# Causal attention scores from two rounded parts and two stacked heads, with the stacks loaded through GpSimd's queue

## What is computed

```python
x = x + attn(layernorm(x))
# in attn, for each of 4 batches and 16 heads
q = (xn @ wq + bq) ; k = (xn @ wk + bk) ; v = (xn @ wv + bv)
scores = einsum('bhqd,bhkd->bhqk', q, k) / sqrt(16)     # 1024 x 1024 a head
attn = softmax(scores + causal_mask)
out = einsum('bhqk,bhkd->bhqd', attn, v) @ wo + bo
```

## Time and profile before

| | us |
|---|---|
| median of 3 runs | 2358.67 (2347.09 to 2362.86) |
| the profiled execution | 2356.39 |
| its span, first to last instruction | 2354.7 |
| prepare | 0 to 195 |
| causal_attention | 195 to 769 |
| one group in its steady part | 32.9 |
| mean granted TensorE clock | 0.952 of 2.4 GHz |

### The profile page before, as it was taken

The page is one execution under the profiler, slowest core; times in us unless marked ns, Lnnn a source line. Parts: engine busy times, 40 slices in busy tenths (PEclk is TensorE's granted clock), DMA queues, the critical chain, the costliest instruction groups (busy, mean ns, idle before and its releaser), DMA issues.

```text
span 2354.7 us, 36114 instructions
## 1 busy us (share of the span) xinstructions
PE 2015.3 (86%) x11968; PEld 1253.7 (53%) x11968; DVE 1448.2 (62%) x3942; ACT 1241.8 (53%) x2980; POOL 798.6 (34%) x663
## 2 busy tenths in 40 slices
PE   5566899999988736989989989989989989989988
PEld 3232233333322525666666666656767667657666
DVE  5467677787774435646646746646745745746744
ACT  1121566666667224745754754753754754754663
POOL 2233221112232335505505505614613613613620
PEclk9796899999999868999999999999999999999999
DMA  5646744554530541000000000011100000000000
GB/s 145 153 132 134 141 98 66 82 82 69 103 109 10 158 138 77 1 28 10 1 23 14 1 23 14 1 66 64 49 19 19 19 19 18 19 4 33 19 1 27
DMA packets 124455, 128.97 MB, mean 55 GB/s; under 512 B 50460, under 2 KB 101232, under 8 KB 123248
## 3 DMA queue, kind: packets, MB, share of 16 engines
q1 hardware_dynamic: 123696, 117.75, 21.6%
q0 software_dynamic: 576, 8.91, 1.0%
HBM read 75.51 MB, written 50.86 MB: 54 GB/s over the span
## 4 chain that ended last, share of the span: by engine, by line
PE 35%; DVE 13%; ACT 8%; issue 6%; POOL 2%; DMA 0%; DVEq 0%; SPq 0%; POOLq 0%; ACTq 0%
DVE rot_s L1862 5%; PE qkv_ps L1372 5%; PE s_ps L1412 4%; PE qkv_ps L1313 4%; PE s_ps L1359 3%; PE pt_ps L1425 3%; PE s_ps L1493 3%; PE o_ps L1450 3%; DVE p_sb L1871 3%; ACT p_sb L1605 2%; POOL inv_norm L1756 2%; PE pt_ps L1412 2%; PE o_ps L1412 2%; PE pt_ps L1493 2%; PE o_ps L1493 2%
## 5 line engine op out<-in xcount | busy, mean ns | idle before, releaser
L699 ACT ACTIVATE probs<-st_ps 128x512 f32<-128x512 f32 (+3 forms) x768 | 327.9, 495 | 185.9 <-PE st_ps L614 184.4
L1313 PE MATMUL qkv_ps<-w_qkv,x_parts 128*128 128x512 f32 x1152 | 309.2, 412 | 33.4 <-DVE x_parts L1836 24.1
L744 DVE CUSTOM_DVE_ANT_0 seen<-s_ps,causal 128x128 f32<-128x128 f32 (+3 forms) x512 | 234.8, 485 | 90.1 <-PE s_ps L599 89.9
L1605 ACT ACTIVATE p_sb<-p_sb,negmax 128x256 f32<-128x256 f32 (+1 forms) x512 | 249.5, 490 | 71.4 <-DVE negmax L1871 71.1
L599 PE MATMUL s_ps<-k_stack,q_stack 96*128 96x512 bf16 (+3 forms) x768 | 244.7, 348 | 42.0 <-DVE piece_negmax L744 20.5
L1313 PEld LDWEIGHTS qkv_ps<-w_qkv,x_parts 128*128 128x128 f32 x1152 | 212.0, 194 | 81.2 <-issue 39.5
L614 PE MATMUL st_ps<-q_stack,k_stack 98*128 98x512 bf16 (+3 forms) x768 | 235.1, 337 | 19.0 <-ACT probs L699 14.4
L1871 DVE CUSTOM_DVE_ANT_0 p_sb<-s_ps,band 128x256 f32<-128x256 f32 (+1 forms) x512 | 185.5, 401 | 89.9 <-PE s_ps L1359 85.2
L1621 ACT COPY p_t<-pt_ps 128x512 f32<-128x512 f32 (+1 forms) x256 | 143.6, 561 | 162.5 <-PE pt_ps L1425 161.1
L821 POOL TENSOR_SCALAR_AFFINE_SELECT probs<-probs 128x512 f32<-128x512 f32 x128 | 81.6, 637 | 433.0 <-ACT probs L699 433.0
L1764 POOL TENSOR_TENSOR rot_c<-qn,turn_by 128x512 f32<-128x512 f32 x128 | 178.6, 1415 | 137.8 <-PE turn_ps L1339 111.9
(11 more groups left out here) (146 smaller groups left out, 3505.1 us busy)
## 6 DMA issues: line engine op xcount, KB each, us to landing
qk_scratch<-parts SPq DMA_DIRECT2D x64, 192.0 KB, 2.8
q_stack<-qk_scratch SPq DMA_DIRECT2D x96, 128.0 KB, 6.7
k_stack<-qk_scratch SPq DMA_DIRECT2D x96, 128.0 KB, 7.1
w_ffn<-ffn_weights POOLq DMA_DIRECT2D x4, 2176.0 KB, 11.7
v_scratch<-v_out SPq DMA_DIRECT2D x32, 256.0 KB, 2.6
v_sb<-v_scratch SPq DMA_DIRECT2D x16, 512.0 KB, 10.0
x_in<-xt_scratch SPq DMA_DIRECT2D x16, 512.0 KB, 4.1
ffn_weights<-w_high SPq DMA_DIRECT2D x2, 2176.0 KB, 7.6
```

Of the source, the lines that this page charges most:

```text
L699: act.activation(probs[:, n % 3, h, q0:CH], st_ps[i % 3][:, q0:CH], ACT.Exp).then_inc(exp_done.sem, 1)
L744: dve.tensor_tensor_reduce(seen[:, i % 3, 0:kw], s_ps[i % 3][:, 0:kw], causal[:, CH - kw:CH], -1.0, BIG, ALU.add, ALU.min, result).then_in ...
L1313: mm = pe.matmul(qkv_ps[:, part * CH:(part + 1) * CH], x_parts[:, w % XR, xp, k, :], w_qkv[:, wp, k, part * INNER:(part + 1) * INNER], sta ...
L1605: act.activation(p_sb[:, u % 4, h, k0:PW], p_sb[:, u % 4, h, k0:PW], ACT.Exp, scale=-1.0, bias=negmax[:, u % 4, h:h + 1], accum_out=total[ ...
```

## The change

Each of q and k is rounded to TensorE's reduced float32 form (`F32R`, four bytes), and the remainder is the second part, so there are two parts of four bytes in place of three of two. `TERMS` has three pairs, so a head needs 48 rows (50 with the shift). Heads 0 and 2 of a group lie in partitions 0 to 49 and heads 1 and 3 in 64 to 113; the order of the pieces alternates between the two heads of a half (`piece_at`). In prepare the second part is one subtraction on GpSimd; VectorE's mid and low go. The rows of ones are written at the start of prepare for 2 x 32 partitions. Stacks and shifts are now issued by GpSimd: the first stack in batch 1 of prepare, the second at the start of causal_attention, the third and fourth behind the first shifts and ahead of group 0's masks, each later one behind the mask of n = 3, the shift of half 0 ahead of the mask of n = 8 and that of half 1 ahead of n = 10. SyncE keeps v, the outputs and the weights. A stack is still 12 DMAs of 128 KB; the shifts are still two DMAs a half.

```diff
-TERMS = ((0, 0), (0, 1), (0, 2), (1, 0), (1, 1), (2, 0))
+TERMS = ((0, 0), (0, 1), (1, 0))
 STK = len(TERMS) * HD1
+ROWS = P // 2
...
+            for side in range(2):
+                pool.dma_start(stack[side * ROWS + r * HD1:side * ROWS + (r + 1) * HD1, slot, :, :],
+                               a["qk_parts"][which, g, part].rearrange("(j b d) t -> b d j t", b=2, d=HD1)[side])\
+                    .then_inc(stack_in[slot], 16)
...
-        rest = sb("rest", [P, 4, CH])
-        parts = sb("parts", [P, 4, 3, CH], BF16)
+        parts = sb("parts", [P, 4, 2, CH], F32R)
...
-            def mid_low(b, i):
-                dve.wait_ge(rest_ready.sem, rest_ready.of(b, i))
-                dve.tensor_copy(parts[:, i % 4, 1, :], rest[:, i % 4, :]).then_inc(mid_ready.sem, 1)
-                dve.wait_ge(mid_ready.sem, mid_ready.of(b, i))
-                dve.tensor_tensor(parts[:, i % 4, 2, :], rest[:, i % 4, :], parts[:, i % 4, 1, :],
-                                  ALU.subtract).then_inc(low_ready.sem, 1)
...
+            for side in range(2):
+                if side:
+                    pool.wait_ge(ones_drawn, 1)
+                pool.memset(as_float(stacks[1][side * ROWS + ROWS // 2:(side + 1) * ROWS]), 1.0).then_inc(ones_drawn, 1)
...
-                    pool.wait_ge(low_ready.sem, low_ready.of(b, i - 4))
-                    pool.tensor_tensor(rest[:, i % 4, :], full[:, i % 4, :], parts[:, i % 4, 0, :],
-                                       ALU.subtract).then_inc(rest_ready.sem, 1)
+                    pool.tensor_tensor(parts[:, i % 4, 1, :], full[:, i % 4, :], as_float(parts[:, i % 4, 0, :]),
+                                       ALU.subtract).then_inc(low_ready.sem, 1)
+                    if b == 1 and i == TC:
+                        for s in parts_stored:
+                            pool.wait_ge(s, 32 * (NI // 4 + 1))
+                        load_stack(pool, a, stacks, 0)
...
+def piece_at(i):
+    half, n, side = i // (NP * HALF), i % (NP * HALF) // HALF, i % HALF
+    return (half * HALF + side,) + PIECES[n]
...
-                pe.matmul(st_ps[i % 3][:, q0:CH], k_stack[0:STK + SHIFT, slot, h, kt * P:(kt + 1) * P],
-                          q_stack[0:STK + SHIFT, slot, h, c * CH + q0:(c + 1) * CH],
+                rows = slice(h % 2 * ROWS, h % 2 * ROWS + STK + SHIFT)
+                pe.matmul(st_ps[i % 3][:, q0:CH], k_stack[rows, slot, h // 2, kt * P:(kt + 1) * P],
+                          q_stack[rows, slot, h // 2, c * CH + q0:(c + 1) * CH],
...
+            def first(group):
+                spread_shift(group, 0)
+                spread_shift(group, 1)
+                for g in range(2, SLOTS):
+                    load_stack(pool, a, stacks, g)
+                pool.wait_ge(bias_in, 16)
+
             def group_work(group, previous, following):
                 for n in DIAGONAL:
+                    if following and n == DIAGONAL[TC]:
+                        spread_shift(following, 0)
+                    if following and n == DIAGONAL[TC + 2]:
+                        spread_shift(following, 1)
...
+                        upcoming = group[0] * SLOTS + group[1] - 1 + SLOTS
+                        if SLOTS <= upcoming < B * NG:
+                            load(upcoming)
```

More of the change, by code:

```diff
@@ L531, in store @@
                              att[:, c].rearrange("p t h d -> p t (h d)")).then_inc(att_stored[c], 16)
-            def spread_shift(g, half):
-                sp.wait_ge(shift_copied.sem, when(shift_copied, (g // SLOTS, g % SLOTS), 2, half))
-                for part in range(SHIFT):
-                    sp.dma_start(q_stack[STK + part:STK + part + 1, g % SLOTS, half * HALF:(half + 1) * HALF, :],
-                                 shift_sb[part * HALF * NT:(part + 1) * HALF * NT, half, :]).then_inc(shift_in[half], 16)
             def load_ffn_weights(l):
@@ L814, in low_parts, with spread_shift, load @@
                         .then_inc(w_low_done.sem, 1)
+            def spread_shift(group, half):
+                pool.wait_ge(shift_copied.sem, when(shift_copied, group, 2, half))
+                for side in range(2):
+                    pool.dma_start(q_stack[side * ROWS + STK:side * ROWS + STK + SHIFT, group[1], half, :],
+                                   shift_sb[side * SHIFT * NT:(side + 1) * SHIFT * NT, half, :])                        .then_inc(shift_in[half], 16)
+            def load(g):
+                pool.wait_ge(pv_done.sem, when(pv_done, (g // SLOTS - 1, g % SLOTS), NS, NS - 1))
+                load_stack(pool, a, stacks, g)
[3 more added lines that the diff above has]
+                for g in range(2, SLOTS):
+                    load_stack(pool, a, stacks, g)
+                pool.wait_ge(bias_in, 16)
             def group_work(group, previous, following):
                 for n in DIAGONAL:
+                    if following and n == DIAGONAL[TC]:
+                        spread_shift(following, 0)
+                    if following and n == DIAGONAL[TC + 2]:
+                        spread_shift(following, 1)
                     q0 = first_query(*SETS[n])
@@ L2075, in build @@
             with ExitStack() as inner:
[L2076 removed]
+                stacks = [inner.enter_context(nc.sbuf_tensor(name, [P, SLOTS, HG // 2, T], F32R))
                           for name in ("q_stack", "k_stack")]
                 stacks.append(inner.enter_context(nc.sbuf_tensor("v_sb", [P, SLOTS, NT, HG * VW], F32)))
[L2079 removed]
+                for name in ("stack_in", "values_in"):
+                    stacks.append([inner.enter_context(nc.semaphore(f"{name}{s}")) for s in range(SLOTS)])
                 prepare(nc, x_all, stacks, ident, neg_half, passed, a)
```

87 lines of the change are left out of this document (35 added, 52 removed).

## The result

The changed kernel takes 2606.5 us (median of 4 runs, 2596.93 to 2615.92) and the kernel before 2359.96: the ratio is 1.106, 95% interval 1.099 to 1.112. It is slower by 10.6%, where 2295 was forecast. The profiled execution took 2614.63 us. I read it as the span was read before: first by slices of it, from the page of the changed kernel (each digit is a tenth, PEclk the granted clock).

A forecast was written before the change was run, and what follows sets the result against it. It took VectorE's work, waits for TensorE and a tail to bound a causal_attention group, and VectorE or stores of v to pace prepare. Terms +5 - 32 - 9 + 7 - 34 = -63 gave 2295 us, range 2250 to 2350.

The forecast's parts named there:

- E, fifteen groups: Causal_attention's steady groups: paired heads run side by side and TensorE is ready earlier, -2.3 us a group, -34 in all.
- attention unchanged: Rival: VectorE and the tail hold a causal_attention group at 32.9 us whatever TensorE does, total 2329; chance 0.12.
- A, rows of ones: Start of prepare: two memsets of 6.9 us each on GpSimd, no longer fully hidden, +5 us.
- C, first stack: Prepare: the first stack's load leaves the queue where v's stores wait, -9 us, ends -14 and +4.
- B, split in prepare: Prepare's half batches: mid and low parts leave VectorE, -4.0 us in each of eight, -32, ends -50 and -12.
- the rival that prices the stores: Rival "Prepare bound by stores": B gives only -12 and C 0, total 2324; chance 0.12.
- D, group 0: Start of causal_attention: 24 stack issues on GpSimd delay group 0's first mask, +10; with group 1's wait covered, +7.
- GpSimd too late: Rival: issues over 1.2 us make the mask of n = 8 late in every group, about 2450 at 1.8; chance 0.06.
- No side by side: Rival: the halves stay apart in causal_attention and TensorE pays weight loads, 3.5 us a group, total 2382; chance 0.07.

The follow-up runs named there:

- the version with and without 32 rows of zeros: Kernel before with two bfloat16 parts, four products, first stack on ScalarE's queue; with zeros up to row 96 2302.94 us, without them (64 and 66 rows) 2614.74 us.
- the exponentials twice: Kernel before with every exponential computed twice, the first time into a tile nobody reads: 2585.84 us.
- three terms one by one: Kernel before with three of its six products, bfloat16, heads one after the other over 48 and 50 rows, rows of ones set at prepare's start: 2597.22 us.
- one by one over 128 rows: Changed kernel with each score matmul over all 128 partitions, float32r, both heads of a pair summed, exponential scaled by a quarter: 2420.04 us.
- The version with two parts of two bytes: Kernel before with two bfloat16 parts, the change's split, four products, zeros up to row 96, first stack on ScalarE's queue: 2302.94 us.
- over 128 rows in bfloat16: Changed kernel with each score matmul over all 128 partitions, and parts and stacks in bfloat16 instead of float32r: 2373.3 us.
- the two runs that differ in the queue alone: Changed kernel over 128 rows in bfloat16, with stacks and shifts issued by GpSimd 2373.3 us, by SyncE as in the kernel before 2343.95 us.

## Why the prediction was wrong

**The step that failed** is E, fifteen groups: the time of TensorE's work. E took a matmul's cost from the earlier trace rows, 0.22 us for 512 columns at a granted clock of 1.00, and let it stand while the change halved the rows of every score matmul. What the runs showed instead is the same work at a mean clock of 0.53: TensorE is busy 49.74 us in the group shown where it was busy 30.39, and it, not VectorE, now sets the group's length. The forecast was -2.3 us a group, and +17.3 was measured (32.9 to 50.1 over ten groups). That the fall comes with the rows is shown by the version with and without 32 rows of zeros, 32.9 and 54.2 us a group.

The clock does stand in the prediction, in one sentence that was never priced: "if the granted clock, 1.00 in the group now, falls when TensorE has more idle time". It is in the list of what would make the prediction wrong and had neither a time nor a chance, and its condition was only half right: idle time does lower the clock (0.85 with the exponentials twice), but in three terms one by one the clock fell with TensorE busy 98.7%. The price could have been worked out from before's rows. TensorE is busy 30.4 of 32.9 us a group; at half the speed that is 60.8 us, less what pairs save. It came to 50.1, as some of the time is still at the upper level. Three terms one by one, without pairs and float32r, are at 50.0: by the estimates above, what pairs save (5.6) is mostly taken back by what float32r costs (3.8), and the rows alone bring the group to where it is.

*Evidence that misled.* The earlier trace rows were rightly read for pairs (64 rows, side by side), but not for the clock: in the 1.25 us of these eight matmuls it was 0.53. These are the stretches view's numbers for them in the kernel before:

```profile
1097.80:1099.05 1.25, 1.25 (x10) 1.01 (x10) 1.25 (x3) 0.00 (x0) 0.49 (x2) 0.53 0.00 0
```

That does not show that they lowered it: it stands in a stretch of 600 us at 0.98, and the fall came 2 us before them. They stand among others over 128 rows, and nothing there told what a whole stage of few rows would do.

Would E have come true at the upper level? An estimate from the runs: 36.8 a group with one by one over 128 rows, less 3 (half of what pairs save at the lower level), is 33.8, no better than 32.9. So E was wrong in more than the clock, and by this estimate "attention unchanged" was nearer than -2.3 a group. Float32r's 1.7 and GpSimd's queue's 1.0 were sized at 0.2 and 0.5, and only about half of the matmuls found a neighbour to run beside.

Term by term:

- *A, rows of ones*, +5: +4.3. The two fills take 13.89 us together, in float32 as in bfloat16 (the run over 128 rows), so elements count and not bytes, nor partitions: 0.85 ns an element over 32 partitions, 0.84 over two in the earlier trace rows. GpSimd's timeline of the changed kernel:

```profile
3.24 13.89 POOL L281 MEMSET k_stack<- 32x8192 f32 x2 [0.56 <-POOLq L2076]
17.44 0.25 POOL L287 TENSOR_SCALAR var_eps<-mean_var 128x8 f32<-128x8 f32 x1 [0.31 <-POOL k_stack L281]
```

- *C, first stack*, -9 (-14 to +4): -9.0 in the profile and -14.0 timed, when done alone. The longest wait for a store of v falls from 18.1 to 8.7 in the changed kernel.

- *B, split in prepare*, -32, with -12 as the end "if the DMA engines, which get 256 KB for every 192, are what holds a half batch": if the first stack is worth the same 9.0 there as alone, the changed kernel got -20.8 - 4.3 + 9.0 = -16, near that end. The version with two parts of two bytes got -44.2 + 9.0 = -35. And in 128 rows one by one, where nothing but the type differs, the first piece comes at 188.31 with float32r and at 170.73 with bfloat16, 17.6 us apart, where two executions of the same prepare differ by 2 (174.82 and 176.80). So the work that leaves VectorE is worth what the term says, and the wider parts take half of it back. B was mis-sized by 16 us, and the rival that prices the stores, at 0.12, was nearer for it. VectorE's waits in prepare, first in the changed kernel, then over 128 rows in bfloat16, show where: the waits for stores are 12 us longer with float32r and in all the same as the 51.6 of the earlier trace rows, while those for `full`, 15.8 in the kernel before, grow with either type.

```profile
DVE v_out L236 <- DMA v_scratch<-v_out: 52.0, 16, 8.7
DVE parts L242 <- ACT full L325: 36.4, 18, 4.3
```

```profile
DVE v_out L236 <- DMA v_scratch<-v_out: 39.6, 16, 6.5
DVE parts L242 <- ACT full L328: 33.8, 20, 3.8
```

- *D, group 0*, +10 there: +7.9 by the two runs that differ in the queue alone. "GpSimd too late" was rightly unlikely: an issue costs 0.51 to 0.57 us, the 12 behind n = 3 end 17 us before the mask of n = 8 (10 us in the shorter group of the run over 128 rows), and the mask of n = 10 starts behind two issues, all as forecast. GpSimd's timeline:

```profile
581.22 1.07 POOL L90 DMA_DIRECT2D q_stack<-qk_parts  x2
...
586.19 1.05 POOL L90 DMA_DIRECT2D k_stack<-qk_parts  x2
...
604.38 0.64 POOL L833 TENSOR_SCALAR_AFFINE_SELECT probs<-probs 128x512 f32<-128x512 f32 x1 [12.19 <-ACT probs L691]
...
611.91 1.12 POOL L810 DMA_DIRECT2D q_stack<-shift_sb  x2 [2.92 <-ACT shift_sb L683]
613.03 0.65 POOL L833 TENSOR_SCALAR_AFFINE_SELECT probs<-probs 128x512 f32<-128x512 f32 x1
```

"No side by side" was wrong in its mechanism, since the pairs are there, if only for about half of the matmuls; its slower weight loads are there too. A range built only from terms at a fixed clock could not hold the time.

## What to carry to other kernels

Before making matmuls smaller, ask what they do to the clock, and give "the clock falls" a time (the stretch's TensorE work at 1.2 GHz) and a chance of its own. A kernel bound by another engine may be holding TensorE's clock up with rows that look wasted; the 32 rows of zeros cost TensorE nothing here (303.86 us busy in ten groups, as in the kernel before) and were worth more than any saving. When a value gets fewer parts but wider ones, count the bytes that are stored, not the parts. And when matmuls are to run side by side, count how many have a neighbour that is ready at the same time.

## What was not expected of the hardware

- The clock depends on rows as well as on busy time. At 98.7% busy over 48 and 50 rows it was at 0.55; at 92% over 96 and 98 rows at 1.00; at 81% over 96 and 98 at 0.85. No run has a number of rows between 66 and 96, so these runs do not say how many are enough. The Trainium skill, TensorE: Matmul & The Clock Gate, Part 1 (the clock gate), has the clock set by how busy the engine has been recently. The traces of this case agree in so far as idle time lowers it, and differ in that a busy engine with few rows stays at 1.2 GHz for hundreds of microseconds (518 in the changed kernel).
- Rows of zeros count (0.57 without them, 1.00 with them), and two matmuls side by side count for more than one by one (0.54 for one half, 0.73 for pairs).
- A weight load of 48 rows in float32r takes 314 ns in the mean, mostly at the lower level, and in bfloat16 130. The loads are busy 15.8 us a group more (304.49 and 146.19 us in ten groups); by the estimate above some 3.8 of these show in the time.
- With two subtractions an item on GpSimd, VectorE's conversions from SBUF take 707 ns in the mean instead of 417, so 29.5 of the 41.3 us that were moved to GpSimd came back on VectorE.
